# One weight transfer moved to ScalarE's queue, and a warm-up of more and narrower matmuls, in a one-core adaLN-FFN kernel

## The chip, the cores and the metric

The kernel runs on one core of one Trainium2 chip. The metric is the device time of one execution in microseconds (us), lower being better; the comparison uses the median over runs. A profiled execution gives the trace from which the rows below are read. Engines: TensorE (PE, with PEld for its weight loads), VectorE (DVE), ScalarE (ACT), GpSimd (POOL) and SyncE (SP), which here only issues DMA transfers. SPq is SyncE's own instruction queue.

## What is computed

x has shape (2, 1024, 256). Each token is viewed as 4 components of 64 lanes. It is filtered with a spectral gate that is the same at all frequencies, and so is a factor per lane, and rotated by two quaternions (one from the condition, one a parameter). Then comes one expert of a feed-forward layer, weighted with its softmax probability, and x is added:

```python
x_right   = hamilton(x_filtered, conj(normalize(q_right)))
r         = hamilton(normalize(cond_256), x_right)      # linear in x, per lane
probs     = softmax(r @ Wr.T)
h         = gelu(r @ W1[7] + b1[7])                     # 256 -> 1024
y         = (h @ W2[7] + b2[7]) * probs[:, 7:8]         # 1024 -> 256
out       = x + y
```

## The kernel before

The rotation is linear in x, so the kernel folds it into the weights: W1 (and the router's matrix) are multiplied by the 256 x 256 rotation matrix, and then x itself goes through the product. The 2048 tokens go in four blocks of 512. All products are made in split precision: an operand is split into a rounded high part and a low rest (w1_hi, w1_lo, xT_hi, xT_lo, h_hi, h_lo), and three products are summed. Each engine has its own hand-written order of instructions, and semaphores tie them together.

The start is what the change touches:

- SyncE issues, in this order: the quaternions (L213, `quats`, 33 KB), the first quarter of W1 together with the router's matrix (L214, `w1_first`, 264 KB, w_first in the profile), x of the first block in two halves of 256 KB (L217), the rest of W1 (L218, 768 KB), W2 in four pieces (L221), the second block of x in another layout (L225), and b2.
- VectorE writes zero into `warm` (L329), makes a small pattern, waits for the quaternions, and computes the unscaled rotation `R_raw` (L357). GpSimd makes the identity matrix `ident` and later the norms' power.
- ScalarE waits for `warm_zeroed` (L271) and runs a GELU on one column (L272), which brings its table load with it. Its next work is the high part of x.
- TensorE runs WARM_UP = 6 fp32 matmuls of a 128 x 128 zero matrix with 128 columns of zeros (L550), whose result nobody reads. Each appears in the trace as two instructions. Then `first_fold` (L556) waits for R_raw and w1_first and multiplies them, 264 columns, two matmuls. Then eight transposes of x (L696), four for each half, each half behind its own DMA. Then `opening`, 24 products of 256 columns (L597), then three more folds of W1 (L568), and from there the main loop over four blocks.
- After the first fold VectorE scales and splits w1_hi (L389) and w1_lo (L394); after the transposes of a half ScalarE takes xT_hi (L281) and VectorE xT_lo (L383). The opening waits for w1_hi and for xT_hi of the first half; its later products wait for w1_lo, for xT_hi of the second half and for xT_lo.

An order in time on TensorE: warm-up, first fold, transposes of the first half, transposes of the second, opening, folds, main loop. It never goes out of this order.

Of the kernel before, what the change touches and what calls it, by code (L numbers as in the profile page):

```python
# [13 lines left out]
P = 128  # L14
# [24 lines left out]
def adaln_ffn(nc, x, small, W1_first, W1_rest, W2, b2, out):  # L39
# [15 lines left out]

    SINGLE = 5
    N_QUAT = 4 + 16 + 1
    WARM_UP = 6

    N_CHUNKS = F // CHUNK  # L60
    W2_TILES = 2
# [7 lines left out]
    with ExitStack() as ctx:  # L69
        def sb(name, shape, dt=F32):  # L70
            return ctx.enter_context(nc.sbuf_tensor(name, shape, dt))

        def sem(name):
            return ctx.enter_context(nc.semaphore(name))
# [25 lines left out]
        w1_first = sb("w1_first", [P, KC, CHUNK + NE])  # L100
# [38 lines left out]
        lT_bank = ctx.enter_context(nc.psum_tensor("lT_bank", [P, 512], F32))  # L139
# [13 lines left out]
        w1_loaded = [sem(f"w1_loaded{i}") for i in range(2)]  # L153
# [49 lines left out]
        def chunk(i):  # L203
            return slice(i * CHUNK, (i + 1) * CHUNK)

        def store(engine, j):

            engine.wait_ge(y_ready, TT * LAST + j + 1)
            engine.dma_start(out_blocks[LAST, :, j, :], y[:, j, :]).then_inc(stored, 16)

        @block.sync
        def _(sp):
            sp.dma_start(quats[:, :], small).then_inc(q_loaded, 16)  # L213
            sp.dma_start(w1_first[:, :, :], W1_first).then_inc(w1_loaded[0], 16)  # L214
            for i in range(2):
                tiles = slice(i * TT // 2, (i + 1) * TT // 2)
                sp.dma_start(x_in[:, tiles, :], x_blocks[0, :, tiles, :]).then_inc(first_x_loaded[i], 16)  # L217
            sp.dma_start(w1_rest[:, :, :], W1_rest).then_inc(w1_loaded[1], 16)  # L218
            for i in range(FT // W2_TILES):
                tiles = slice(i * W2_TILES, (i + 1) * W2_TILES)  # L220
                sp.dma_start(w2[:, tiles, :], W2[i]).then_inc(w2_loaded[i], 16)  # L221

            def load_squares(b):
                for q in range(QUADS):
                    sp.dma_start(x_sq[q * SQ:(q + 1) * SQ, :, :], x_squares[b, q]).then_inc(x_sq_loaded, 16)  # L225

            load_squares(1)
            sp.dma_start(b2_all[:, :], b2.to_broadcast([P, C])).then_inc(b2_loaded, 16)
            for b in range(N_BLOCKS):
                if b > 0:  # L230

                    sp.wait_ge(y_ready, TT * b)
                    sp.dma_start(out_blocks[b - 1], y[:, :, :]).then_inc(stored, 16)
                if b + 2 < N_BLOCKS:

                    sp.wait_ge(x_turned, KC * (b + 1))
                    load_squares(b + 2)
                if b < LAST:

                    sp.wait_ge(rest_ready, TT * (b + 1))  # L240
                    sp.dma_start(x_in[:, :, :], x_blocks[b + 1]).then_inc(x_loaded, 16)
            for j in range(0, TT, 2):
                store(sp, j)
            sp.wait_ge(stored, 16 * (LAST + TT))
# [24 lines left out]
        @block.scalar  # L269
        def _(act):  # L270
            act.wait_ge(warm_zeroed, 1)  # L271
            nc.scalar.activation(gelu_scratch[:, :], warm[:, :], ACT.Gelu)  # L272

            def split_x(b, k):

                act.wait_ge(x_turned, KC * (b - 1) + k + 1)
                nc.scalar.activation(xT_hi[b % 2][:, k, :], xT[b % 2][:, k, :], ACT.Copy).then_inc(xT_hi_ready, 1)  # L277

            def split_first_x(half):
                act.wait_ge(first_x_turned, half + 1)  # L280
                nc.scalar.activation(xT_hi[0][:, :, half * HALF:(half + 1) * HALF], xT_ps[half],  # L281
                                     ACT.Copy).then_inc(xT_hi_ready, 1)

            def split_w1(i):
                act.wait_ge(folded, KC * (i + 1))
                nc.scalar.activation(w1_hi[:, :, chunk(i)], fold_banks[i], ACT.Copy).then_inc(w1_hi_ready, 1)

            def copy_first_x(half):

                act.wait_ge(xT_lo_ready, half + 1)  # L290
                nc.scalar.activation(xT[0][:, :, half * HALF:(half + 1) * HALF], xT_ps[half],
                                     ACT.Copy).then_inc(xT_copied, 1)

            def gelu(b, f):
                act.wait_ge(pre_done, FT * b + f + 1)

                if f >= SLOTS:
                    act.wait_ge(acc_done, (FT - 1) * b + f + 1 - SLOTS)
                elif b > 0 and f == SLOTS - 1:
                    act.wait_ge(tile_done, TT * b)  # L300
                elif b > 0:
                    act.wait_ge(acc_done, (FT - 1) * (b - 1) + FT + f + 1 - SLOTS)
                s = f % SLOTS
                nc.scalar.activation(h_hi[:, s, :], pre[f % 2][:, :], ACT.Gelu,  # L304
                                     bias=b1_cols[:, f:f + 1]).then_inc(h_hi_ready, 1)
                if b == 0 and f == 0:
                    split_w1(1)
                nc.scalar.activation(h_all[:, s, :], pre[f % 2][:, :], ACT.Gelu,  # L308
                                     bias=b1_cols[:, f:f + 1]).then_inc(h_ready, 1)

            for half in range(2):
                split_first_x(half)
            for half in range(2):
                copy_first_x(half)
            for b in range(N_BLOCKS):
                for f in range(FT):
                    gelu(b, f)
                    if b == 0 and f == 0:
                        split_w1(2)
                        split_w1(3)  # L320
                    if f == 4 and b < LAST:
                        for k in range(KC):
                            split_x(b + 1, k)
            for j in range(1, TT, 2):
                store(act, j)
# [221 lines left out]
        def _(pe):  # L547
            zeros = nc.const_aps.tensor(0.0, [P, P], F32)
            for _ in range(WARM_UP):
                nc.tensor.matmul(lT_bank[:, 0:P], zeros, zeros, start=True, stop=True)  # L550

            def first_fold():

# [209 lines left out]
```

## Time and profile before

| | |
|---|---|
| median of 3 runs | 106.59 us (106.47 to 107.71) |
| the profiled execution, its own time | 105.98 us |
| its span, from the first instruction to the last | 104.2 us |
| TensorE busy | 100.1 us, 96% of the span |
| VectorE, ScalarE, GpSimd busy | 66.5, 48.9, 25.7 us |
| mean granted TensorE clock | 0.997 of full speed |

Reading it: busy times of engines overlap, so they don't add up to the span. TensorE is busy nearly always, and the others wait for it more than it for them. A start time in a row is counted from the beginning of the span. For matmuls the start printed is that of their issue; the duration includes the way through the array, so that consecutive ones overlap in the rows, and the distance of two starts is the pace at which they stream.

### The profile page before, as it was taken

To read this page: it belongs to the slowest core of one execution; us is meant where nothing else is said; L and a number is where in the kernel's file an instruction comes from. 1 tells how busy PE (TensorE), PEld (TensorE's weight loads), DVE (VectorE), ACT (ScalarE), POOL (GpSimd) and SP (SyncE) were. 2 spreads that over 40 slices of the span, in tenths; PEclk is the share of its full clock that TensorE was granted. 3 is DMA by queue.
4 is the path that set the end of the run, shared out by engine and by line. 5 is a ranking of instruction groups with operands and counts; after the bars stand their busy time and mean duration, and the time that the engine had idled before them with its cause. 6 is when DMAs were issued, how large, how long until landed. Compare 5 with 4: busy or idle time off the path is not lost.

```text
span 104.2 us, 1505 instructions
## 1 busy us (share of the span) xinstructions
PE 100.1 (96%) x572; PEld 84.9 (82%) x572; DVE 66.5 (64%) x143; ACT 48.9 (47%) x79; POOL 25.7 (25%) x16
## 2 busy tenths in 40 slices
PE   7899999999999999999999999999999999999990
PEld 7679888878888888888888878788888878888980
DVE  1599589878264999288224997272494972378451
ACT  5046794444441484484424544834424544442700
POOL 3400000029999300000000000069998000000000
PEclk9999999999999999999999999999999999999998
DMA  1999910170004222350600050000006040000005
GB/s 25 287 388 369 178 26 6 42 159 0 0 0 123 88 101 101 74 127 0 200 2 3 0 208 0 0 0 0 0 0 201 6 201 0 0 0 0 0 5 196
DMA packets 9222, 8.12 MB, mean 78 GB/s; under 512 B 6784, under 2 KB 7424, under 8 KB 9216
## 3 DMA queue, kind: packets, MB, share of 16 engines
q1 hardware_dynamic: 8928, 7.78, 25.4%
q10 hardware_dynamic: 288, 0.26, 0.7%
q8 instruction: 4, 0.07, 0.3%
q14 instruction: 2, 0.02, 0.1%
HBM read 5.94 MB, written 2.10 MB: 77 GB/s over the span
## 4 chain that ended last, share of the span: by engine, by line
PE 91%; DMA 4%; SPq 1%; DVE 1%; DVEq 0%; issue 0%
PE pre L627 40%; PE acc L634 25%; PE acc L642 15%; DMA x_in<-in_x 4%; PE pre L597 3%; PE lT_bank L586 2%; PE acc L638 1%; PE acc L636 1%; DVE y L462 1%; PE extra L568 1%; PE acc L568 1%; PE lT_bank L568 1%; PE acc L696 1%; SPq L217 0%; SPq L214 0%; DVEq L69 0%
## 5 line engine op out<-in xcount | busy, mean ns | idle before, releaser
L304 ACT ACTIVATE h_hi<-pre,quats 128x512 fp32r<-128x512 f32 x32 | 22.1, 690 | 43.5 <-PE pre L627 42.5
L428 DVE TENSOR_TENSOR h_lo<-h_all,h_hi 128x512 fp32r<-128x512 f32 x32 | 21.8, 690 | 20.1 <-ACT h_all L308 19.8
L634 PE MATMUL acc<-w_parts,h_hi 128*128 128x512 f32 x116 | 32.3, 391 | 0.0
L634 PEld LDWEIGHTS acc<-w_parts,h_hi 128*128 128x128 f32 x116 | 21.5, 188 | 4.5
L627 PE MATMUL pre<-xT_hi,w_hi 128*128 128x512 f32 x60 | 24.0, 400 | 0.0
L627 PE MATMUL pre<-xT_lo,w_hi 128*128 128x512 f32 x60 | 23.7, 394 | 0.0
L642 PE MATMUL acc<-w_parts,h_lo 128*128 128x256 f32 x128 | 23.0, 283 | 0.0
L266 POOL TENSOR_TENSOR exps<-e_const,shifted 128x32 f32<-128x32 f32 x4 | 22.2, 5577 | 0.2
L642 PEld LDWEIGHTS acc<-w_parts,h_lo 128*128 128x128 f32 x128 | 20.0, 189 | 2.7 <-DVE h_lo L428 0.7
L308 ACT ACTIVATE h_all<-pre,quats 128x512 f32<-128x512 f32 x32 | 21.8, 683 | 0.0
L627 PE MATMUL pre<-xT_hi,w_lo 128*128 128x512 f32 x60 | 18.7, 392 | 0.0
L261 POOL TENSOR_TENSOR shifted<-logits_wide,logit_max 128x64 f32<-128x64 f32 x2 | 1.3, 672 | 52.0 <-DVE logit_max L435 52.0
L627 PEld LDWEIGHTS pre<-xT_hi,w_lo 128*128 128x128 f32 x60 | 11.3, 188 | 2.6
L627 PEld LDWEIGHTS pre<-xT_hi,w_hi 128*128 128x128 f32 x60 | 11.3, 188 | 2.1 <-issue 0.4
L627 PEld LDWEIGHTS pre<-xT_lo,w_hi 128*128 128x128 f32 x60 | 11.3, 189 | 1.6
L457 DVE SCALAR_TENSOR_TENSOR part<-acc,prob,rest 128x256 f32<-128x256 f32 x16 | 7.4, 477 | 5.8 <-PE acc L642 5.7
L462 DVE SCALAR_TENSOR_TENSOR y<-acc,prob,part 128x256 f32<-128x256 f32 x16 | 7.6, 483 | 1.5 <-PE acc L642 1.0
L452 DVE SCALAR_TENSOR_TENSOR rest<-b_all,prob,x_in 128x256 f32<-128x256 f32 x16 | 6.9, 481 | 0.1
L420 DVE STREAM_TRANSPOSE xT<-x_sq 128x512 f32<-128x512 f32 x6 | 6.1, 1090 | 0.0
L377 DVE TENSOR_TENSOR xT_lo<-xT,xT_hi 128x512 fp32r<-128x512 f32 x6 | 4.1, 717 | 0.0
L550 PE MATMUL lT_bank<-const-float32-0.0 128*128 128x128 f32 x12 | 2.9, 432 | 0.8 <-PEq L756 0.8
L277 ACT ACTIVATE xT_hi<-xT 128x512 fp32r<-128x512 f32 x6 | 3.4, 630 | 0.0
(68 smaller groups left out, 59.3 us busy)
## 6 DMA issues: line engine op xcount, KB each, us to landing
x_sq<-in_x SPq DMA_DIRECT2D x12, 128.0 KB, 3.6
x_in<-in_x SPq DMA_DIRECT2D x3, 512.0 KB, 3.4
out<-y SPq DMA_DIRECT2D x3, 512.0 KB, 2.6
w<-in_W SPq DMA_DIRECT2D x4, 256.0 KB, 6.3
w_rest<-in_W_rest SPq DMA_DIRECT2D x1, 768.0 KB, 5.8
x_in<-in_x SPq DMA_DIRECT2D x2, 256.0 KB, 3.9
w_first<-in_W_first SPq DMA_DIRECT2D x1, 264.0 KB, 2.7
out<-y SPq DMA_DIRECT2D x2, 128.0 KB, 1.7
```

The lines of the kernel that those rows point to most:

```text
L266: nc.gpsimd.tensor_tensor(exps[i][:, :, :], e_const[:, :].unsqueeze(2).to_broadcast([P, TT, NE]), shifted[:, i * TT:(i + 1) * TT, :], ALU. ...
L304: nc.scalar.activation(h_hi[:, s, :], pre[f % 2][:, :], ACT.Gelu, bias=b1_cols[:, f:f + 1]).then_inc(h_hi_ready, 1)
L308: nc.scalar.activation(h_all[:, s, :], pre[f % 2][:, :], ACT.Gelu, bias=b1_cols[:, f:f + 1]).then_inc(h_ready, 1)
L377: nc.vector.tensor_tensor(xT_lo[b % 2][:, k, :], xT[b % 2][:, k, :], xT_hi[b % 2][:, k, :].bitcast(F32), ALU.subtract).then_inc(xT_lo_read ...
L420: nc.vector.transpose(xT[b % 2][:, k, :].rearrange("p (j t s) -> p j s t", j=TT, s=QUADS), x_sq[:, :, k::KC].rearrange("p (s j) c -> p j s ...
L428: nc.vector.tensor_tensor(h_lo[:, s, :], h_all[:, s, :], h_hi[:, s, :].bitcast(F32), ALU.subtract).then_inc(h_lo_ready, 1)
L452: nc.vector.scalar_tensor_tensor(out=rest[:, j, :], in0=b2_all[:, :], scalar=prob[:, j:j + 1], in1=x_in[:, j, :], op0=ALU.mult, op1=ALU.ad ...
L457: nc.vector.scalar_tensor_tensor(out=part[:, j, :], in0=acc_low[j], scalar=prob[:, j:j + 1], in1=rest[:, j, :], op0=ALU.mult, op1=ALU.add) ...
L462: nc.vector.scalar_tensor_tensor(out=y[:, j, :], in0=acc_high[j], scalar=prob[:, j:j + 1], in1=part[:, j, :], op0=ALU.mult, op1=ALU.add).t ...
L627: last = nc.tensor.matmul(bank[:, :], w[:, k, cols], part_of_x[:, k, :], start=(n == 0), stop=(n == len(steps) - 1))
L634: nc.tensor.matmul(acc[j][:, :], rows, w2_parts[:, f, :, :], start=(f == 0), stop=False)
L642: return nc.tensor.matmul(acc_high[j], h_lo[:, f % SLOTS, j * P:(j + 1) * P], w2_parts[:, f, 0, :], start=False, stop=(f == FT - 1 or (b = ...
```

## The change

Three lines are touched. The transfer of `w1_first` is taken from SyncE's list and issued on ScalarE, behind its wait for `warm_zeroed` and ahead of the GELU of one column. The warm-up becomes 15 matmuls with 64 columns each, still of a 128 x 128 stationary matrix: 15 x 64 = 960 columns in place of 6 x 128 = 768, and 30 weight loads in place of 12. Semaphores and everything else stay.

```diff
-    WARM_UP = 6
+    WARM_UP = 15
...
         def _(sp):
             sp.dma_start(quats[:, :], small).then_inc(q_loaded, 16)
-            sp.dma_start(w1_first[:, :, :], W1_first).then_inc(w1_loaded[0], 16)
             for i in range(2):
...
         def _(act):
             act.wait_ge(warm_zeroed, 1)
+            act.dma_start(w1_first[:, :, :], W1_first).then_inc(w1_loaded[0], 16)
             nc.scalar.activation(gelu_scratch[:, :], warm[:, :], ACT.Gelu)
...
             for _ in range(WARM_UP):
-                nc.tensor.matmul(lT_bank[:, 0:P], zeros, zeros, start=True, stop=True)
+                nc.tensor.matmul(lT_bank[:, 0:P // 2], zeros, zeros[:, 0:P // 2], start=True, stop=True)
```

On SyncE, from the program's start, the kernel before issues these:

```order
1 L213 DMA quats<-in_small 128x66
2 L214 DMA w_first<-in_W_first 128x528
3 L217 DMA x_in<-in_x 128x512 x2
4 L218 DMA w_rest<-in_W_rest 128x1536
5 L221 DMA w<-in_W 128x512 x4
6 L225 DMA x_sq<-in_x 32x16x64 x4
```

and the changed one these (its line numbers are lower by one from there on):

```order
1 L213 DMA quats<-in_small 128x66
2 L216 DMA x_in<-in_x 128x512 x2
3 L217 DMA w_rest<-in_W_rest 128x1536
4 L220 DMA w<-in_W 128x512 x4
5 L224 DMA x_sq<-in_x 32x16x64 x4
```

Both halves of x, and all behind them, stand one place earlier. On TensorE, from the start, the difference of the two orders is this (x15 counts matmuls, each of two passes in the trace):

```order
 L546 UNCONDITIONAL_BRANCH
-L550 MATMUL lT_bank<-const-float32-0.0 128x128 x6
+L550 MATMUL lT_bank<-const-float32-0.0 128x64 x15
 L556 MATMUL acc<-w_first,R_raw 128x264 x2
 L696 MATMUL acc<-ident,x_in 128x128 x8
```

Nothing on TensorE moved; the warm-up ahead of the fold has other steps.

## Rows read from the trace of the kernel before

**Rows 1.** The page's busy times: busy us, share of the span, instructions.
```profile
PE 100.1 (96%) x572; PEld 84.9 (82%) x572; DVE 66.5 (64%) x143; ACT 48.9 (47%) x79; POOL 25.7 (25%) x16
```

**Rows 2.** PE by stretch: us, sum, busy (instructions), granted clock, DMA share, GB/s.
```profile
7.00:12.00 5.00, 5.00 (x35) 1.00 1.17 311
...
70.00:100.00 30.00, 30.00 (x164) 1.00 0.10 36
```

**Rows 3.** The chain that ended last, first 13 us: start us, us, what.
```profile
1.18 0.42 SPq L214
...
1.64 0.43 SPq L217
...
2.12 4.17 DMA x_in<-in_x
...
6.33 0.75 PE acc L696 x4
7.07 3.01 PE pre L597 x24
```

**Rows 4.** PE in order of time: start us, us, line, operation, count, idle before.
```profile
0.77 2.90 PE L550 MATMUL lT_bank<-const-float32-0.0 128*128 128x128 f32 x12 [0.77 <-PEq L756]
...
1.12 0.63 PE L550 MATMUL lT_bank<-const-float32-0.0 128*128 128x128 f32 x2
...
3.25 0.42 PE L550 MATMUL lT_bank<-const-float32-0.0 128*128 128x128 f32 x1
...
4.60 0.39 PE L556 MATMUL acc<-w_first,R_raw 128*128 128x264 f32 x1
...
5.04 0.39 PE L556 MATMUL acc<-w_first,R_raw 128*128 128x264 f32 x1
```

**Rows 5.** PE's weight loads in order of time.
```profile
0.74 0.29 PEld L550 LDWEIGHTS lT_bank<-const-float32-0.0 128*128 128x128 f32 x1 [0.74 <-issue]
...
0.91 0.33 PEld L550 LDWEIGHTS lT_bank<-const-float32-0.0 128*128 128x128 f32 x1
...
4.19 0.34 PEld L556 LDWEIGHTS acc<-w_first,R_raw 128*128 128x128 f32 x1
...
5.46 0.19 PEld L696 LDWEIGHTS acc<-ident,x_in 128*128 128x128 f32 x1 [0.44 <-issue]
...
5.55 0.34 PEld L696 LDWEIGHTS acc<-ident,x_in 128*128 128x128 f32 x2
```

**Rows 6.** Who waited for whom, first 13 us: us in total, times, longest.
```profile
PEld acc L696 <- issue: 0.4, 1, 0.4
PEld acc L696 <- DMA x_in<-in_x: 0.3, 1, 0.3
```

**Rows 7.** Issue to landing: w_first (its only transfer), then both halves of x.
```profile
DMA to landing us min/median/max: 2.7/2.7/2.7
...
DMA to landing us min/median/max: 3.7/3.9/4.2
```

**Rows 8.** Stretches of the start: sum, busy of PE PEld DVE ACT POOL, clock, DMA share, GB/s.
```profile
2.00:3.00 1.00, 1.00 (x6) 1.00 (x6) 0.38 (x5) 0.22 (x2) 0.00 (x0) 1.00 0.62 121
3.00:4.00 1.00, 0.67 (x4) 0.38 (x2) 0.80 (x6) 0.00 (x0) 0.56 (x1) 1.00 0.89 240
4.00:5.00 1.00, 0.94 (x3) 0.87 (x4) 0.21 (x2) 0.00 (x0) 0.72 (x1) 1.00 0.94 320
```

**Rows 9.** ScalarE and VectorE in order of time, first 8 us.
```profile
0.73 1.28 ACT L272 ACT_TABLE_LOAD   x1 [0.73 <-PEq L756]
...
3.41 0.43 DVE L357 TENSOR_TENSOR R_raw<-lane_eye,M 128x256 f32<-128x256 f32 x1
...
5.15 0.88 DVE L389 TENSOR_SCALAR w_hi<-acc,scale 128x256 fp32r<-128x256 f32 x2
...
5.94 0.87 DVE L394 SCALAR_TENSOR_TENSOR w_lo<-acc,scale,w_hi 128x256 fp32r<-128x256 f32 x2
...
6.25 0.60 ACT L281 ACTIVATE xT_hi<-acc 128x512 fp32r<-128x512 f32 x1 [4.02 <-PE acc L696]
```

## Prediction

> **What bounds the kernel now.** I read the page first: TensorE (PE) is busy 96% of the span [rows 1]. The busy times of PE by stretch then show that every stretch from 7 us up to 100 us is full [rows 2], and by the waits of PE nothing after the fold waits. So whatever happens behind 7 us is carried through: a change of the opening moves the end by exactly as much as it moves the first product of the opening, and by nothing else. The chain of waits over the first 13 us says what sets that moment: three DMA issues on SyncE, the landing of the second half of x (2.12 + 4.17 = 6.29 us), four transposes, then the 24 products of the opening in one run from 7.07 us [rows 3].
>
> That chain names only the last wait. Read beside it PE and its weight loads, instruction by instruction. In these rows a matmul streams from about the moment at which the next weight load starts. The warm-up's 12 passes (an fp32 matmul is two passes) start 0.213 us apart ((3.25 - 1.12) / 10), the first really at 0.91, so the last stops streaming at about 3.46 [rows 4, 5]. The fold (L556) needs R_raw, done at 3.84 us [rows 9], and w_first, landed at 1.18 + 2.7 = 3.88 [rows 3, 7]: both at once. It streams from 4.19 [rows 5] to about 5.26 (last start 5.04 plus 0.22) [rows 4]. Then PE's weight loads idle 0.44 us, and the transposes of x's first half begin at 5.46, streaming from 5.55 [rows 5]; that half landed at 1.64 + 3.7 = 5.34 [rows 3, 7]. ScalarE takes xT_hi from them at 6.25 to 6.85, and the first product starts at 6.96 (streaming 7.07). The 0.31 us for which PE then waited for x's second half [rows 6] therefore nearly coincides with another wait, that for ScalarE: shortening the second landing alone gives at most 0.1 us. What counts is when the transposes of the FIRST half start.
>
> **The clock.** The granted clock reads 1.00 in all stretches. Yet a 128-column warm-up pass takes 0.213 us and a 264-column fold pass 0.22 us (5.04 - 4.82, read as half of the step from 4.60 to 5.04) [rows 4]: the first is the pace of 1.2 GHz, the second that of 2.4. The first fold pass, 4.19 to 4.60, takes 0.41; at 1.2 GHz all through it would take 0.44. So the clock rose at about 4.57, after a warm-up, a gap of 0.73 us and most of one pass. A denser warm-up could at best make the whole fold run at the high level: 0.41 - 0.22 = 0.19 us.
>
> **The change, part by part.**
> SyncE no longer issues w_first, so both halves of x are issued 0.46 us earlier (1.64 - 1.18) [rows 3]. If the transfers take as long as now, the first half lands at 4.88 and the second at 5.83. PE is then free of both: transposes can stream right behind the fold, at 5.26 instead of 5.57 (5.46 plus the 0.1 between load and stream). Gain 0.31 us. Work behind it that could hold it back: VectorE finishes w1_hi at 5.15 + 0.88 = 6.03, before the new first product at 6.65, and w1_lo at 5.94 + 0.87 = 6.81, needed at 7.1 [rows 9]; ScalarE is idle before xT_hi. These cost nothing; without that cover they would cost up to the same 0.31. Everything queued on SyncE behind (w_rest, W2, squares, b2) moves forward too and is needed later; nothing in it becomes late.
>
> ScalarE issues w_first behind its wait for the memset of `warm` (over at about 0.87 us), so at about 0.95, 0.2 us earlier than 1.18. The issue takes 0.34 to 0.42 us of the queue, and pushes the table load of 1.28 us [rows 9] to about 2.65; the next work on ScalarE is at 6.25, so it is free. Landing: with 2.7 us as now, 3.65. But w_first no longer has the engines ahead of x: two queues are served at once. At 0.03 + 0.26 + 0.26 MB (quaternions, w_first, and as much of x), and with about 0.03 MB moved before 2 us and 121, 240 and 320 GB/s in the next three [rows 8], the last byte lands at 4.54, less the 0.28 by which it all starts earlier: 4.26. So w_first lands between 3.65 and 4.26. At 3.65 R_raw still holds the fold at 4.19. At 4.26 it streams from about 4.46; 0.11 us of the first pass is then at the low level and the rest at the high one, and it ends 0.14 us later. I take a value between, 0.1.
> The Trainium skill ("DMA: Bandwidth & Descriptors", Rules for kernel authors) says that spreading transfers over the issuing engines does not help bandwidth, since all run on the same 16 DMA engines, and saves only sequencer issue time. By that rule the gain on the x side is the issue time only, which is what the sum has.
>
> The warm-up becomes 15 matmuls of 64 columns, 30 passes. The unknown is the price of a pass. Half the columns of a 0.213 us pass are 0.107 us: 30 of them from 0.91 end at 4.11, just before the fold's 4.19; no cost. But every pass still loads 128 x 128 fp32 weights. The rows bound that load from above twice: it hides behind 0.213 us now, and from idle the second load follows the first by 0.17 us (0.91 - 0.74), where at the high clock it follows by 0.09 (5.55 - 5.46) [rows 5]. So a pass costs between 0.107 and 0.165 us at the low clock. The 0.165 contains the start from idle, which a stream need not pay; I take the lower end, not with much confidence. If the load bounds it, PE executes warm-up while the fold is ready, and all of it lies on the path. Break-even with the 0.31 is at about 0.125 us a pass.
> The Trainium skill speaks against the change here: "TensorE: Matmul & The Clock Gate" (LDWEIGHTS, and Back-to-back issue gap) gives a load as the stationary columns over 1.2 GHz, and a sustained stream of load and matmul pairs of 128 columns as 81 ns where the matmul alone is 56. By the first figure a 64-column pass is just even with its load, by the second the load shows; no row here has such a pass.
>
> Sum: 0.31 gained, 0.1 given back by w_first: 0.2 us. The profiled execution took 105.98 us (span 104.2 and 1.8 around it) and would be 105.8; the median of the runs shown is 0.61 above it, and 106.59 - 0.2 = **106.4 us**.
>
> **Rivals.**
> A, the above: 106.4, within 106.1 (all 0.31 and the 0.19 of the clock) and 106.6.
> B, the weight loads bound the warm-up, and the fold starts late. At 0.165 us, 22 passes end at 4.54, where the clock rises; 8 more at 0.09 end at 5.26. The fold runs 5.3 to 6.18 instead of ending at 5.26: 0.92 late, less 0.31 since x is there: +0.6, 107.2 us. At the worst, 0.213 us a pass, 17 passes by 4.57 and 13 at 0.107 end at 5.96, the fold at 6.84, +1.3, 107.9 us. It decides from 0.125 us a pass on. For it: the load interval of 0.17 from idle, and the size of the load, unchanged. Against: that interval includes a start. This is the case on the other side.
> C, no net change: w_first lands later than 4.3, or the 0.44 us before the transposes, which the profile puts down to issue and not to the DMA [rows 6], is not the landing but something behind the fold that stays. 106.6 us. Against: the landing at 5.34 fits.
> D, B and in addition the clock stays low past the fold, because PE spends part of each step waiting for weights instead of streaming. Fold from 5.86 (0.91 + 30 x 0.165), 4 x 0.44 to 7.62, first four transposes at 0.213 to 8.47, ScalarE 0.6 and 0.2 of hand-over: first product at 9.3 instead of 7.07, +2.2 us, 108.8. Nothing in the trace speaks for it but the gap of 0.73 us, over which the clock rose all the same.
>
> **The numbers.** A 0.50, B 0.31, C 0.14, D 0.05. The range: 106.1 less 0.2 for the spread of the lower runs shown is 105.9; at the top it takes in B's usual price and a little over, 107.5, and leaves out D and B's worst. A's own range is 105.9 to 106.8. A difference over 2% (2.1 us, about what a measurement of this kernel can tell from no change) on the fast side no case gives: 0.02 for what I haven't seen. On the slow side D and a tail of B: 0.06. Within: 0.92.
>
> **What would show it.** Warm-up passes starting 0.11 us apart and the last ended by 4.2: A; 0.12 to 0.17 and the fold's first load behind 4.3: B. ScalarE's issue of w_first near 0.95 and w_first landed by 4.26. SyncE's issues of x at 1.18 and 1.64, landings near 4.9 and 5.8. Transposes beginning within 0.1 us of the fold's last pass, no idle of weight loads for x; if 0.3 to 0.4 us of idle stay there, C. Opening products from about 6.85 and a span near 104.0. Fold passes all of 0.22 us show that the clock rose before the fold. The prediction is wrong if the first product starts after 7.1, or if PE waits anywhere behind 7 us.

## The result, and the profile after

The changed kernel is slower: 109.98 us median (109.59 to 110.03, 4 runs) against 106.53 (105.54 to 107.71) for the kernel before, a ratio of 1.035 with a 95% interval of 1.027 to 1.042. The profiled execution has a span of 108.2 us, 4.0 more than before. The comparisons leave out executions more than 1.5% above the fastest of their kernel; medians and lowest and highest times given here are of all.

The chain of waits of the changed kernel over its first 17 us (start us, us, what) answers to [rows 3]:

```profile
0.77 6.64 PE lT_bank L550 x30
7.41 1.87 PE acc L556 x4
9.28 1.71 PE acc L696 x8
10.98 3.14 PE pre L597 x24
14.12 0.86 PE lT_bank L568 x4
```

No transfer stands in it any more. TensorE runs warm-up for 6.64 us, and the run of 24 products begins at 10.98 instead of 7.07 us: 3.91 of the 4.0 us. That run itself takes 3.14 us where it took 3.01, which is the rest. Behind it nothing changed; by stretch TensorE is as full as in [rows 2] (us, sum, busy, clock, DMA share, GB/s):

```profile
11.00:16.00 5.00, 5.00 (x34) 1.00 0.59 78
16.00:50.00 34.00, 34.00 (x198) 1.00 0.23 63
50.00:100.00 50.00, 50.00 (x280) 1.00 0.12 43
```

The weight loads one by one answer to [rows 5]; a matmul streams from about the start of the next load, so their distances are the pace:

```profile
0.91 0.34 PEld L550 LDWEIGHTS lT_bank<-const-float32-0.0 128*128 128x128 f32 x1
1.12 0.34 PEld L550 LDWEIGHTS lT_bank<-const-float32-0.0 128*128 128x128 f32 x1
...
6.89 0.33 PEld L550 LDWEIGHTS lT_bank<-const-float32-0.0 128*128 128x128 f32 x1
7.10 0.33 PEld L556 LDWEIGHTS acc<-w_first,R_raw 128*128 128x128 f32 x1
7.31 0.33 PEld L556 LDWEIGHTS acc<-w_first,R_raw 128*128 128x128 f32 x1
7.75 0.34 PEld L556 LDWEIGHTS acc<-w_first,R_raw 128*128 128x128 f32 x1
...
10.14 0.23 PEld L696 LDWEIGHTS acc<-ident,x_in 128*128 128x128 f32 x1
10.35 0.23 PEld L696 LDWEIGHTS acc<-ident,x_in 128*128 128x128 f32 x1
...
11.04 0.24 PEld L597 LDWEIGHTS pre<-xT_hi,w_hi 128*128 128x128 f32 x1
11.21 0.19 PEld L597 LDWEIGHTS pre<-xT_hi,w_hi 128*128 128x128 f32 x1
11.33 0.19 PEld L597 LDWEIGHTS pre<-xT_hi,w_hi 128*128 128x128 f32 x1
```

Two things are to be seen. A pass of 64 columns costs (6.89 - 1.12) / 27 = 0.214 us, as much as one of 128 columns did (0.213). And the pace of 1.2 GHz lasts: fold passes take 0.44 us (7.75 - 7.31) and transposes 0.21 (before 0.12, from 5.55 on), and only behind 11.04 do the loads come down to 0.12 apart. The granted clock again reads 1.00 everywhere, as before; these distances are what shows the level. It rose at about 11.1 us, before the change at 4.57. A rise is placed like this from here on: a distance that lies between the slow and the fast one is split into a slow and a fast part; the trace's stored records of the clock, where it has any, agree to 0.03 us, and place it where it falls into a gap (last section).

The transfers did what they were meant to (issue on ScalarE, then issue to landing of w_first and of the halves of x; the issues on SyncE are at 1.18 and 1.65):

```profile
0.90 0.37 ACTq L271 DMA_DIRECT2D w_first<-in_W_first  x1
...
DMA to landing us min/median/max: 2.8/2.8/2.8
...
DMA to landing us min/median/max: 3.7/4.1/4.4
```

w_first is there at 3.7 us, x at 4.9 and 6.0. Nobody takes them before 7.3.

### The profile page after: what moved, and what is told of

The parts are those of the page before. It is cut to its first block, busy times and chain, and to the rows that moved or that the text cites. A ratio compares the mean times of both kernels' runs of the same rounds, so it can differ in the third digit from the quotient of the medians.

```text
span 108.2 us, 1541 instructions
## 1 busy us (share of the span) xinstructions
PE 104.7 (97%) x590; PEld 89.8 (83%) x590; DVE 66.5 (61%) x143; ACT 48.9 (45%) x79; POOL 25.7 (24%) x16
## 4 chain that ended last, share of the span: by engine, by line
PE 96%; DVE 1%; DVEq 0%; issue 0%
PE pre L627 39%; PE acc L634 24%; PE acc L642 14%; PE lT_bank L550 6%; PE pre L597 3%; PE lT_bank L586 2%; PE acc L556 2%; PE acc L696 2%; PE acc L638 1%; PE acc L636 1%; DVE y L462 1%; PE lT_bank L568 1%; PE acc L568 1%; PE extra L568 1%; DVEq L69 0%
## 5 line engine op out<-in xcount | busy, mean ns | idle before, releaser
L550 PE MATMUL lT_bank<-const-float32-0.0 128*128 128x64 f32 x30 | 6.6, 422 | 0.8 <-PEq L756 0.8
L550 PEld LDWEIGHTS lT_bank<-const-float32-0.0 128*128 128x128 f32 x30 | 6.5, 332 | 0.7 <-issue 0.7
L281 ACT ACTIVATE xT_hi<-acc 128x512 fp32r<-128x512 f32 x2 | 1.2, 597 | 7.6 <-PE acc L696 7.6
```

Of the source, the lines that this page charges most:

```text
L550: nc.tensor.matmul(lT_bank[:, 0:P // 2], zeros, zeros[:, 0:P // 2], start=True, stop=True)
```

## The experiments

Two theories stood after the result. L: only the length of the warm-up costs (30 passes, each bound by its weight load). S: on top of it the half-empty passes keep the clock down for longer. The runs came in three groups, each on a chip of its own, and the kernel before was run beside each; its medians were 106.25 us (queue move alone, six narrow, fifteen wide, narrow weights), 106.47 (seven wide, eight wide, eight narrow, the warm-up alone) and 106.55 (no warm-up, eight wide on SyncE, 96 columns). A ratio is to the kernel before of the same group.

**The queue move alone.**

```diff
# against the changed kernel
-    WARM_UP = 15
+    WARM_UP = 6
-                nc.tensor.matmul(lT_bank[:, 0:P // 2], zeros, zeros[:, 0:P // 2], start=True, stop=True)
+                nc.tensor.matmul(lT_bank[:, 0:P], zeros, zeros, start=True, stop=True)
```

> The changed kernel with the old warm-up (6 matmuls of 128 columns): only the transfer is moved. Theory (all of the loss is the warm-up's, and the queue move does what was worked out): w_first lands by 3.8 us, the fold starts where it did or 0.1 earlier, the transposes of x's first half follow the fold without the 0.44 us of idle, first product 0.2 to 0.4 us earlier than before, 106.2 us against 106.5. Rival (the queue move takes part in the loss, or brings nothing): first product not earlier than 6.96, 106.5 us or more.

Measured: 106.01 us (105.58 to 108.05, 12 runs), ratio 0.9985 (0.995 to 1.002). The loss is gone without the new warm-up, and the queue move by itself costs nothing that shows. The chain of waits:

```profile
1.64 4.33 DMA x_in<-in_x
6.02 0.75 PE acc L696 x4
6.77 3.02 PE pre L597 x24
```

The second half of x lands at 5.97 instead of 6.29, and the products start 0.30 us earlier, near the 0.31 worked out. The fold streams from 4.26 rather than 4.19, because in this execution the quaternions landed later (2.1 us after their issue, before 1.9) and R_raw with them. But the fold took 1.16 us in it and not 1.37, the clock having risen before it, so part of the 0.30 is the clock's. In the times the gain is not distinguished from none.

**Six narrow matmuls**, in the kernel before:

```diff
# against the kernel before
-                nc.tensor.matmul(lT_bank[:, 0:P], zeros, zeros, start=True, stop=True)
+                nc.tensor.matmul(lT_bank[:, 0:P // 2], zeros, zeros[:, 0:P // 2], start=True, stop=True)
```

> The kernel before with 6 warm-up matmuls of 64 columns instead of 128; the transfer stays on SyncE. As a pass costs 0.213 us for its weight load whatever its columns, the warm-up lasts as long as before, to 3.46 us. Only the columns streamed in it are half as many. Theory S (the clock comes late because each pass streams half the time): fold passes take 0.44 us and transposes 0.21, the low pace holds for 3 us or more longer than before, and the time is 1 to 2 us above before. Theory L (only the length of the warm-up cost time): the same as before, 106.5 us, the clock rising in the fold.

Measured: 107.42 us (106.92 to 108.11, 4 runs), ratio 1.013 (1.008 to 1.018): 1.2 us above the kernel before. TensorE in order of time:

```profile
0.77 2.79 PE L550 MATMUL lT_bank<-const-float32-0.0 128*128 128x64 f32 x12 [0.77 <-PEq L756]
4.45 2.10 PE L556 MATMUL acc<-w_first,R_raw 128*128 128x264 f32 x4 [0.88 <-DMA w_first<-in_W_first]
6.34 1.91 PE L696 MATMUL acc<-ident,x_in 128*128 128x128 f32 x8
8.18 1.13 PE L597 MATMUL pre<-xT_hi,w_hi 128*128 128x256 f32 x4
```

The warm-up ended when it did before (to 0.1 us), and yet the fold took 2.10 us where it had taken 1.37, and the clock rose in the fourth product, at about 9.1 us. This speaks for S, with one blemish: w_first landed 0.4 us later in this execution.

**Fifteen wide matmuls**, in the changed kernel:

```diff
# against the changed kernel
-                nc.tensor.matmul(lT_bank[:, 0:P // 2], zeros, zeros[:, 0:P // 2], start=True, stop=True)
+                nc.tensor.matmul(lT_bank[:, 0:P], zeros, zeros, start=True, stop=True)
```

> The changed kernel with its 15 warm-up matmuls 128 columns wide. As long as a pass is bound by its weight load these cost no more time than those of 64 columns. Theory S: the clock rises at about 4.5 us, inside the warm-up, the passes behind it take 0.11 us, the warm-up ends near 6 us, the fold near 6.9, first product near 8.2 us and 107.8 us in all. Theory L: 30 passes of 0.213 us all the way, the fold from 7.3 us, 110 us as the changed kernel.

Measured: 108.01 us (107.42 to 108.08, 4 runs). Twice the columns, and 1.97 us faster than the changed kernel (whose times were taken in another group, 109.59 to 110.03). Its TensorE, then its weight loads around the rise:

```profile
0.77 5.49 PE L550 MATMUL lT_bank<-const-float32-0.0 128*128 128x128 f32 x30 [0.77 <-PEq L756]
6.10 1.05 PE L556 MATMUL acc<-w_first,R_raw 128*128 128x264 f32 x4
```

```profile
4.32 0.33 PEld L550 LDWEIGHTS lT_bank<-const-float32-0.0 128*128 128x128 f32 x1
4.54 0.30 PEld L550 LDWEIGHTS lT_bank<-const-float32-0.0 128*128 128x128 f32 x1
4.75 0.20 PEld L550 LDWEIGHTS lT_bank<-const-float32-0.0 128*128 128x128 f32 x1
4.87 0.19 PEld L550 LDWEIGHTS lT_bank<-const-float32-0.0 128*128 128x128 f32 x1
...
5.88 0.19 PEld L550 LDWEIGHTS lT_bank<-const-float32-0.0 128*128 128x128 f32 x1
5.99 0.19 PEld L556 LDWEIGHTS acc<-w_first,R_raw 128*128 128x128 f32 x1
```

The loads still start 0.21 us apart up to 4.75 and 0.12 at 4.87, so the clock rose at about 4.8 us, from where a pass took 0.11 us. L asked for 110 us and falls.

**Narrow weights too**, in the changed kernel:

```diff
# against the changed kernel
-                nc.tensor.matmul(lT_bank[:, 0:P // 2], zeros, zeros[:, 0:P // 2], start=True, stop=True)
+                nc.tensor.matmul(lT_bank[0:P // 2, 0:P // 2], zeros[:, 0:P // 2], zeros[:, 0:P // 2], start=True, stop=True)
```

> The changed kernel with the warm-up's stationary matrix cut to 64 columns too (64 x 64 results), 15 matmuls. If a pass is bound by the load of 128 stationary columns: passes start 0.107 us apart, the warm-up ends at 4.1 us, the fold starts at 4.2 or before, and the time is 106.2 us, as with the queue move alone. If a pass has a fixed price of 0.213 us whatever its weights: 110 us as the changed kernel.

Measured: 106.16 us (105.67 to 106.47, 10 runs). The same 30 passes and the same moving columns, 3.8 us faster than the changed kernel. TensorE, and two neighbouring answers of its weight loads, three loads from 3.58 and the last one at 3.79, which are 0.107 us apart:

```profile
0.77 3.43 PE L550 MATMUL lT_bank<-const-float32-0.0 128*64 128x64 f32 x30 [0.77 <-PEq L756]
4.19 1.82 PE L556 MATMUL acc<-w_first,R_raw 128*128 128x264 f32 x4
```

```profile
3.58 0.44 PEld L550 LDWEIGHTS lT_bank<-const-float32-0.0 128*64 128x64 f32 x3
...
3.79 0.23 PEld L550 LDWEIGHTS lT_bank<-const-float32-0.0 128*64 128x64 f32 x1
```

So the price of the narrow pass in the changed kernel is that of its 128 stationary columns, and not a fixed one. With 64 of them it falls to half; since 64 moving columns can account for 0.107 us by themselves (half of the 0.213 for 128), this is only an upper bound on what a load of 64 columns costs. The pass now has the price that the prediction had given it, and the warm-up ends at about 4.0 us. That the total is only 0.2 us off the 106.4 forecast is not evidence for the forecast's sum: in this profile the clock rose at 5.6 us, the fold took 1.82 instead of 1.37 us, and the first product began at 7.26 instead of 6.99. Nor is a gain shown: the ratio is 0.999 (0.996 to 1.002).

**Eight wide against eight narrow.** Here both warm-ups have 16 passes and end at 4.3 us, where the fold can start. Only the columns differ.

```diff
# eight wide: against the queue move alone
-    WARM_UP = 6
+    WARM_UP = 8
# eight narrow: against the changed kernel
-    WARM_UP = 15
+    WARM_UP = 8
```

> The queue move with 8 warm-up matmuls of 128 columns: 16 passes to 4.3 us, no gap ahead of the fold. To be compared with e7, which has the same 16 passes and half the columns. Theory S: the clock rises in or near the fold; 106.1 us. Theory L has no other number here.

> The changed kernel with 8 warm-up matmuls of 64 columns in place of 15: 16 passes of 0.213 us, ending at 4.3 us as in e6, without a gap ahead of the fold. Theory S: fold and transposes at the low pace, 1.2 to 1.9 us above e6, 107.5 to 108. Theory L (with the length gone the loss is gone): within 0.3 us of e6.

Measured: 105.98 us (105.57 to 106.54, 10 runs) and 106.92 us (106.79 to 107.54, 10 runs), with no overlap. The chain of waits of the wide one, then of the narrow one:

```profile
1.64 5.09 DMA x_in<-in_x
6.78 0.74 PE acc L696 x4
7.52 2.86 PE pre L597 x24
```

```profile
0.77 3.65 PE lT_bank L550 x16
4.42 1.87 PE acc L556 x4
6.29 1.63 PE acc L696 x8
7.92 3.10 PE pre L597 x24
```

In the narrow one the fold and all eight transposes go at 1.2 GHz; the clock rose at about 7.7 us. In the wide one the fold already runs at the high pace (1.13 us). It does so although this execution was held up twice by its transfers: w_first landed at 4.4 us, which left 0.3 us between warm-up and fold, and TensorE then waited 0.6 us for the second half of x. S holds in kind; its size here is 0.94 us, below the 1.2 to 1.9 that was expected.

**96 columns**, between the two, again 16 passes 0.21 us apart:

```diff
# against eight narrow
-                nc.tensor.matmul(lT_bank[:, 0:P // 2], zeros, zeros[:, 0:P // 2], start=True, stop=True)
+                nc.tensor.matmul(lT_bank[:, 0:96], zeros, zeros[:, 0:96], start=True, stop=True)
```

> As e7, with 96 columns per warm-up matmul instead of 64: the same 16 passes of 0.213 us, three quarters of the columns of e6. Theory S: between e6 (105.98) and e7 (106.92), passes 0.213 us apart. If only a pass that is full counts: as e7. If half the loss was the narrow tile itself and not the columns streamed: as e7 too.

Measured: 106.76 us (106.34 to 106.94, 10 runs), ratio 1.006 (1.003 to 1.009). Eight wide had 0.994 (0.990 to 0.999) and eight narrow 1.005 (1.001 to 1.009), in the other group. So 96 columns are slower than 128, and in the times they are not told from 64: whether the loss goes down with the columns, as S says, the times leave open. The one profile, of the second fastest execution, lies between: in it the clock rose at about 5.9 us, as the transposes began, and these took 1.12 us where eight narrow has 1.83:

```profile
4.26 1.89 PE L556 MATMUL acc<-w_first,R_raw 128*128 128x264 f32 x4
5.99 1.12 PE L696 MATMUL acc<-ident,x_in 128*128 128x128 f32 x8
```

**The warm-up alone**, the transfer left on SyncE:

```diff
# against the kernel before
-    WARM_UP = 6
+    WARM_UP = 15
-                nc.tensor.matmul(lT_bank[:, 0:P], zeros, zeros, start=True, stop=True)
+                nc.tensor.matmul(lT_bank[:, 0:P // 2], zeros, zeros[:, 0:P // 2], start=True, stop=True)
```

> The kernel before with the changed warm-up (15 matmuls of 64 columns), the transfer of w_first left on SyncE. Theory: the warm-up hides every landing, since it runs to 7.3 us and w_first and x are there by 6.3; 110.0 us, the same as the changed kernel. Rival (the queue move adds to the loss, or takes from it, under the long warm-up): more than 0.4 us away from 110.0.

Measured: 109.73 us (109.47 to 110.21, 4 runs), ratio 1.030 (1.023 to 1.037), where the changed kernel has 1.035 (1.027 to 1.042). The warm-up edit alone makes the loss; what the move adds to it is within the noise.

**No warm-up**, in the kernel before:

```diff
-    WARM_UP = 6
+    WARM_UP = 0
```

> The kernel before without any warm-up. The fold then is TensorE's first work, at 4.0 us. Theory (a warm-up that streams is what lets the clock rise early): fold, transposes and opening all at the low pace, 0.7 us for the fold, then the 24 products of the opening at 0.21 instead of 0.12 us, 2 us; 107.5 to 109.5 us, more than e7 and less than the changed kernel, which pays 3 us of delay on top. Rival (what ends ahead of the fold does not matter): 106.5 us.

Measured: 107.27 us (107.08 to 107.61, 4 runs), 0.7 us above the kernel before and 2.7 us better than the changed kernel. The ratio is 1.011 (1.005 to 1.017). The lower bound expected, 107.5, was missed: the clock rose at about 8.35 us, in the second product, so only the fold, the transposes and not quite two products were slow. TensorE:

```profile
4.12 2.10 PE L556 MATMUL acc<-w_first,R_raw 128*128 128x264 f32 x4 [4.12 <-DMA w_first<-in_W_first]
6.00 1.92 PE L696 MATMUL acc<-ident,x_in 128*128 128x128 f32 x8
7.84 0.94 PE L597 MATMUL pre<-xT_hi,w_hi 128*128 128x256 f32 x4
```

**Is a warm-up up to the fold worth something?** Seven wide matmuls with the queue move, and eight with the transfer left on SyncE:

```diff
# seven wide: against the queue move alone
-    WARM_UP = 6
+    WARM_UP = 7
# eight wide on SyncE: against the kernel before
-    WARM_UP = 6
+    WARM_UP = 8
```

> The queue move with 7 warm-up matmuls of 128 columns, 14 passes, which end at 0.91 + 14 x 0.213 = 3.9 us, just ahead of the fold. Theory (a warm-up that streams all the time and ends at the fold costs nothing and spares runs in which the clock comes late): median 105.9 us, and no runs near 107.8, which the kernel before and the queue move alone both had among theirs. Rival (when the clock rises has nothing to do with the gap ahead of the fold): the same two groups of times as with 6, median 106.0 to 106.3.

> The kernel before with 8 warm-up matmuls of 128 columns instead of 6, the transfer left on SyncE: e6 without the queue move. If the 0.5 us by which e6 beat the kernel before come from the warm-up that reaches the fold, the median stays within 0.2 us of e6's, and no runs near 107.7. If they come from the queue move, it is as the kernel before, 106.3 to 106.5 us.

Measured: 106.00 us (105.51 to 106.79, 12 runs; ratio 0.999, 0.995 to 1.003) and 106.13 us (105.50 to 107.45, 12 runs; ratio 0.999, 0.995 to 1.004). Neither expectation decides: 106.00 lies on the border of theory (105.9) and rival (106.0 to 106.3). In the one profile of seven wide the theory does not hold: the warm-up ended 0.3 us ahead of the fold, and the clock still rose only at about 6.9 us, so that the fold took 2.13 us:

```profile
0.77 3.32 PE L550 MATMUL lT_bank<-const-float32-0.0 128*128 128x128 f32 x14 [0.77 <-PEq L756]
4.01 2.13 PE L556 MATMUL acc<-w_first,R_raw 128*128 128x264 f32 x4
```

The times near 107.7 that the expectations speak of are absent where they were to be absent (seven wide has none above 106.8, of 12, the kernel before 11 of 29 above 107 beside it), but eight wide on SyncE, which was to have none, has two of 12 at 107.4. No such execution was profiled, so what makes it long is not shown. Eight wide with the queue move is the only kernel whose ratio leaves out 1 on the fast side, 0.9944 (0.9903 to 0.9985). Which of its two parts brings that 0.5 us the runs do not tell, since the same warm-up without the move is not told from the kernel before, nor from eight wide with the move (106.13 and 105.98 us).

## Why the prediction was wrong

The forecast was 106.4 us with a range up to 107.5, and 109.98 was measured; the likeliest case A did not come, and 0.06 was given to the side that did.

- **What bounds the kernel, and that only the first product's start matters: right.** 3.91 of the 4.0 us of span lie ahead of that product, and TensorE is full behind it. ("Nothing after the fold waits" goes too far as a sentence: the transposes wait for x in [rows 6], and the working uses that.)
- **The queue terms: right in kind, small in fact.** Issues at 0.90, 1.18 and 1.65 us; w_first landed at 3.7, at the lower bound of 3.65 to 4.26; x at 4.9 and 6.0 where 4.88 and 5.83 were worked out. The landings vary more than my bounds: with eight wide w_first landed at 4.4 and the second half of x took 5.09 us. (The 0.28 us in the upper bound stands in no row; the 0.2 beside it would have given 4.3.) With the queue move alone the transposes followed the fold directly, so case C's doubt about the 0.44 us of "issue" [rows 6] is settled: it was the landing of the first half. The 0.31 us of gain showed in one trace and not in the times.
- **The step that failed: the price of a pass**, "I take the lower end". It costs 0.213 us, not 0.107. Worse, the upper end of "between 0.107 and 0.165 us" was no bound: the 0.17 us from the first load to the second [rows 5] was read as what a load costs at most, but in a stream of loads of 128 fp32 columns the distance was 0.212 to 0.218 us at this clock. Why the first one is shorter the runs do not show. The sound bound from rows was the 0.213 itself [rows 4], behind which the load was hidden so exactly that it could not be seen. The prediction did price that, as B's worst, at 107.9; fifteen wide passes, in which the clock rose about when B's worst has it rise, measured 108.01. So B's worst is the price of the long warm-up with the clock as before, and the changed kernel took 2 us more than it.
The Trainium skill ("TensorE: Matmul & The Clock Gate", LDWEIGHTS) gives a load as its columns over 1.2 GHz, which is 107 ns for 128 columns. For these fp32 weights the runs say 0.213 us for 128, twice the page's figure, and the measurement decides.
- **The clock, the second error.** The sum let the clock rise at 4.57 us as before and named a late rise only in D, with 0.05. It rose at 11.1 us. With full passes in the same number it rose at 4.8 and the time was 108.01; so of the 3.45 us of loss about 1.5 (108.01 against 106.53, measured in different groups; 1.76 against the 106.25 beside it) go to the length of the warm-up and 1.97 to the late clock. With the length taken away, half-filled passes cost 0.94 us (eight narrow against eight wide). D was the right mechanism at too short a pass: it had 0.165 us and came to 108.8. Put together, the fold began to stream at 7.31 instead of 4.19 (3.1 us), and took 1.76 where it had taken 1.07 (0.7 us).
- **D's "Nothing in the trace speaks for it but the gap of 0.73 us" was an argument from absence.** The kernel before has no half-filled pass, so its trace could neither support nor exclude a late rise. That called for a higher chance than 0.05, and for one tied to B, since in a pass that its load bounds TensorE does not stream all the time.

## What to carry to other kernels

A warm-up matmul is priced by the larger of its stationary and its moving side. Here cutting only the moving columns saved no time (0.213 us a pass with 128, 96 and 64), and the kernels with fewer columns were slower, with the clock at its low level for longer. Keep warm-up passes full, or cut the weights with the columns, and count them so that the last ends where the first real matmul can start: every pass past that is on the path. What a warm-up can earn is little here, 0.7 us between none and the six of the kernel before, and the fifteen narrow ones, which end 3 us after the fold could start, made the kernel 2.7 us slower than no warm-up at all. And where a row's duration is a maximum over two hidden costs, halving one of them tells nothing until the other has been measured by itself.

## What the runs showed of the hardware that was not expected

- A load of 128 fp32 stationary columns binds at 0.213 us per pass at 1.2 GHz, whether 128, 96 or 64 columns are moved. A pass of 64 by 64 takes 0.107, so a load of 64 takes no more than that. At 2.4 GHz passes of 128 by 128 columns follow at 0.11.
- Where the clock rose differs with the warm-up ahead of it. With full passes it was 4.8 us or before in five profiles (before, queue move alone, fifteen wide, both with eight wide) and about 6.9 in one (seven wide, an execution of 106.75 us); with both sides narrow 5.6, with 96 columns 5.9. With half-filled passes it was 7.7, 9.1, 9.2 and 11.1, and 8.35 without any warm-up. Among equal warm-ups it differs by 1.9 us from profile to profile (9.2 and 11.1, both with 30 narrow passes), so a single profile does not give its size.
- The view's granted clock read 1.00 in stretches in which every distance was that of 1.2 GHz. In 11 of the 13 traces the stored records of the clock begin with the rise (4.56 us before the change, 11.14 after it), where the distances put it too; for the time ahead of it they have no entry, and the view then prints 1.00. Two traces (six narrow, eight wide) have no entry at all. The distance of two weight loads is the surer sign.
